# Second fetch behind the weight residues on GpSimd, down casts 2 and 3 one product group later

## Chip, cores and metric

One NeuronCore of a Trainium2 chip runs the whole program. The metric is device microseconds of one execution; lower is better.

## What is computed

Four layers act on x of 4 batches by 512 rows by 512 columns: a graph attention, a mixture of eight experts with two of them for each row, an attention on a normalized score matrix, and a feed-forward layer in which a hidden value survives only if it is among the two largest of its four. The change touches the program of the last two:

```
    def _L1_xattn_ref(p, k_v, W_k, b_k, ln_gamma, ln_beta):
...
        kv = k_v @ W_k.T + b_k
        out = jnp.einsum('bij,bjd->bid', p, kv)
        sim = jnp.einsum('bid,bjd->bij', out, kv) * scale
        mu = jnp.mean(sim, axis=-1, keepdims=True)
        var = jnp.var(sim, axis=-1, keepdims=True)
        sim = (sim - mu) * jax.lax.rsqrt(var + EPS) * ln_gamma + ln_beta
        attn = jax.nn.softmax(sim, axis=-1)
        return attn
...
        h = jax.nn.silu(jnp.einsum('bsh,hi->bsi', x, w_gate)) * jnp.einsum('bsh,hi->bsi', x, w_up)
        h_sparse = _sparsify_2to4(h)
        return jnp.einsum('bsi,ih->bsh', h_sparse, w_down)
    x = x + _L0_xattn_ref(ctx_512, _layernorm(x, axis=-1), L0_xattn_W0, ...)
    x = x + _L0_ffn_ref(_layernorm(x, axis=-1), L0_ffn_gate_w, ...)
    x = x + _L1_xattn_ref(_layernorm(x, axis=-1), ctx_512, L1_xattn_W_k, ...)
    x = x + _L1_ffn_ref(_layernorm(x, axis=-1), L1_ffn_w_gate, ...)
    return x
```

## The kernel before

All matrix products are made of three: each float32 operand is split into a rounded part ("hi", cast on ScalarE) and a residue ("lo", raw minus hi), and TensorE adds hi by lo, lo by hi and hi by hi (`product3`, lines 76 to 78).

The feed-forward layer (`ffn`) runs in 16 **units** n = 0 to 15. A unit is one batch of 512 rows by one quarter of the 2048 hidden columns. In a unit TensorE makes four **product groups** r = 0 to 3, each a gate and an up product for 128 hidden columns (24 matmuls), and then the down product of the unit before, in four row tiles (48 matmuls). Two consecutive units at a batch border use the same quarter, so there are 13 weight sets: units 4, 8 and 12 bring no new one (`starts(n)` is false for them).

A set has four gate/up pieces (512 KB each) and four down pieces (256 KB each). A piece is loaded by SyncE's queue into one of two raw slots, cast on ScalarE (`act_gate_up` line 1391, `act_down` line 1399) and its residue is made on GpSimd (`pool_gate_up` line 1403, `pool_down` line 1409). The residue frees the slot. SyncE issues in the order of its program and waits before each load for the residue two pieces back. In a unit with both kinds its order is: down 2, down 3, next set's down 0, down 1, then gate/up 2, gate/up 3, next set's gate/up 0, 1.

In unit n the down pieces of set `SPLIT[n - 1]` are prepared if unit n - 1 started it, and the gate/up pieces of the set that unit n + 1 starts. So units 1, 2, 4, 6, 8, 10, 12 and 14 prepare both, units 3, 7, 11 and 15 down alone (unit 15 its own set's down pieces too), units 5, 9 and 13 gate/up alone.

On VectorE a unit has the four hidden products (line 1449), then `keep_two` for each half of the rows: ScalarE takes magnitudes (`size`, line 2419), VectorE makes three compares (line 2510), eight tallies (2516 to 2523) and four mask multiplies (2526). Then ScalarE rounds the hidden tiles (2426) and VectorE makes their residues (2532) at the start of the next unit. `evac` (2545) adds a down tile to x.

Between these, the attention of batches 1 to 3 (and the last part of the expert layer for them) is done in halves of 256 rows, by `later`, in slots 6n to 6n + 5 of unit n, under a plan. For half h the steps fall so: in unit 2h - 1, slot 6n + 1 the first fetch of expert rows from DRAM on GpSimd (`fetch(pool, h, 0)`) and in slot 6n + 2 the first add on VectorE and the second fetch into the same buffer, which waits for that add; in unit 2h the second add and the statistics (slot 6n), GpSimd's power for 1/deviation (`pool_rstd`, line 2093), ScalarE's norm (line 2140), TensorE's transposes (line 2115) ahead of group 3, the context product behind group 3 and the similarity product between the halves of the down product; in unit 2h + 1 the score normalization, exponentials (line 2157), the probability add (line 2227), and the second norm and its transposes.

Of the kernel before, what the change touches and what calls it, by code (L numbers as in the profile page):

```python
# [30 lines left out]
Q, RQ = I // (4 * P), 4  # L31
# [2215 lines left out]
def ffn(nc, outer, dram, out):  # L2247
# [3 lines left out]
    with ExitStack() as ctx:  # L2251
# [3 lines left out]
        u, later = outer["units"], outer["later"]  # L2255
# [19 lines left out]
        def due(name, slot):  # L2275
            return plan.get((name, slot), ())

        def starts(n):
            return n < UNITS and FIRST[SPLIT[n]] == n

        with nc.Block() as block:
# [40 lines left out]
            @block.gpsimd  # L2322
            def _(pool):
                def slot_work(slot):
                    for h in due("centre", slot):
                        later.pool_rs(pool, h)
                    for h in due("add1", slot):
                        later.pool_rstd(pool, 0, h)
                    for h in due("prob", slot):
                        later.pool_rstd(pool, 1, h)  # L2330
                    for h in due("fetch0", slot):
                        later.fetch(pool, h, 0)
                    for h in due("add0", slot):
                        later.fetch(pool, h, 1)

                for r in range(2, RQ):
                    u.pool_gate_up(pool, 0, r)
                    slot_work(r - 1)
                slot_work(RQ - 1)
                for r in range(RQ):  # L2340
                    u.pool_gate_up(pool, 1, r)
                for n in range(1, UNITS):
                    down = (SPLIT[n - 1],) if starts(n - 1) else ()
                    gate = (SPLIT[n + 1],) if starts(n + 1) else ()
                    for s in down:
                        u.pool_down(pool, s, 0)
                        u.pool_down(pool, s, 1)
                    slot_work(6 * n)
                    for s in down:
                        u.pool_down(pool, s, 2)  # L2350
                        u.pool_down(pool, s, 3)
                    for s in gate:
                        u.pool_gate_up(pool, s, 0)
                    slot_work(6 * n + 1)
                    for s in gate:
                        u.pool_gate_up(pool, s, 1)
                    slot_work(6 * n + 2)
                    for s in gate:
                        u.pool_gate_up(pool, s, 2)
                    slot_work(6 * n + 3)  # L2360
                    for s in gate:
                        u.pool_gate_up(pool, s, 3)
                if starts(LAST):
                    for r in range(RQ):
                        u.pool_down(pool, SPLIT[LAST], r)
# [32 lines left out]
            def _(act):  # L2398
                def early(slot):
                    for h in due("turn0", slot):  # L2400
                        later.act_hi(act, 0, h)
                    for h in due("context", slot):
                        later.act_o_hi(act, h)
                    for h in due("turn1", slot):
                        later.act_hi(act, 1, h)
# [9 lines left out]
                def size(n, k):  # L2415
                    act.wait_ge(u.hid_made, RQ * (n + 1))
                    if 2 * n + k >= 1:
                        act.wait_ge(mag_free, 2 * n + k)
                    act.activation(mag[:, :, :], hid[:, :, HN * k:HN * k + HN], ACT.Abs).then_inc(mag_ready, 1)  # L2419
# [20 lines left out]
                for n in range(1, UNITS):  # L2440
                    down = (SPLIT[n - 1],) if starts(n - 1) else ()
                    gate = (SPLIT[n + 1],) if starts(n + 1) else ()
                    for r in range(RQ):
                        early(6 * n + r)
                        u.act_silu(act, n, r, sg)
                        if r == 0:
                            round_hid(n - 1)
                        for s in gate:
                            if r >= 1:
                                u.act_gate_up(act, s, r - 1)  # L2450
                        for s in down:
                            if r < 2:
                                u.act_down(act, s, 2 * r)
                                u.act_down(act, s, 2 * r + 1)
                        if n == LAST and starts(n) and r >= 1:
                            u.act_down(act, SPLIT[n], r - 1)
                        late(6 * n + r)
                    early(6 * n + 4)
                    if n == LAST and starts(n):
                        u.act_down(act, SPLIT[n], RQ - 1)  # L2460
                    size(n, 0)
                    for s in gate:
                        u.act_gate_up(act, s, RQ - 1)
                    size(n, 1)
                    early(6 * n + 5)
                for k in range(2):
                    half = slice(HN * k, HN * k + HN)
# [237 lines left out]
```

## Time and profile before

| | |
|---|---|
| median of 3 runs | 1108.22 us (1106.13 to 1113.89) |
| profiled execution | 1109.6 us |
| its span | 1107.9 us |
| TensorE matmul busy | 973.3 us, 88% |
| VectorE busy | 707.0 us, 64% |
| ScalarE busy | 445.8 us, 40% |
| GpSimd busy | 387.1 us, 35% |

Times in the trace are microseconds from the span's start. The feed-forward units run from about 509 us to the end. A row of a timeline names the engine, the line of the kernel, the operation, the tiles written and read, and in brackets how long the engine stood idle before it and who ended that. PE is TensorE, DVE VectorE, ACT ScalarE, POOL GpSimd, SPq SyncE's DMA queue.

### The profile page before, as it was taken

How to read it: one execution, taken by the hardware profiler on the slowest of the kernel's cores; microseconds unless marked ns; L12 is line 12 of the kernel's file. 1: busy time of each engine (PE TensorE's matmuls, PEld its weight loads, DVE VectorE, ACT ScalarE, POOL GpSimd, SP SyncE). 2: the span in 40 equal slices, each digit the busy share in tenths (PEclk: the TensorE clock that was granted, in tenths of full speed). 3: DMA queues.
4: the chain of work that ended last, by engine and by line, in shares of the span. 5: the costliest groups of instructions: out<-in, count | busy, mean ns of one | idle time of the engine just before them, and what ended most of it. 6: DMA issues, size and time to landing. Idle time of an engine off the chain costs nothing.

```text
span 1107.9 us, 15674 instructions
## 1 busy us (share of the span) xinstructions
PE 973.3 (88%) x4615; PEld 806.6 (73%) x4616; DVE 707.0 (64%) x1436; ACT 445.8 (40%) x753; POOL 387.1 (35%) x368
## 2 busy tenths in 40 slices
PE   4996539999999996428698999998999989999997
PEld 3883339999999994216586888877888868888885
DVE  7986734422435223592678796995978959855566
ACT  4875234332434322223344345433443443433431
POOL 0465023341232302232463335244442553143530
PEclk8998759999999997558798999999999999999999
DMA  8267044452444313301341223233212421033211
GB/s 328 66 145 210 38 158 153 165 175 76 147 166 137 95 57 105 114 1 57 98 131 58 85 68 102 70 100 109 77 47 68 153 86 66 13 102 114 76 53 43
DMA packets 46237, 113.85 MB, mean 103 GB/s; under 512 B 7137, under 2 KB 7265, under 8 KB 45025
## 3 DMA queue, kind: packets, MB, share of 16 engines
q1 hardware_dynamic: 37600, 90.03, 24.4%
q0 software_dynamic: 8576, 23.08, 8.0%
q8 instruction: 30, 0.49, 0.2%
q14 instruction: 31, 0.25, 0.1%
HBM read 90.28 MB, written 22.81 MB: 102 GB/s over the span
## 4 chain that ended last, share of the span: by engine, by line
PE 34%; DVE 13%; ACT 2%; POOL 2%; issue 1%; DMA 1%; ACTq 0%; DVEq 0%
PE ps L76 11%; PE ps L78 11%; PE ps L77 11%; DVE raw L2510 3%; DVE f_hid L2526 2%; DVE kv_c_lo L2532 1%; DVE l_stats L2178 1%; DVE x L2168 1%; POOL f_w_lo L1409 1%; DVE x L2227 1%; DVE x L2545 1%; PE ps L2115 1%; DMA raw<-in_ffn_dn 1%; POOL f_w_lo L1403 1%; POOL l_rstd L2093 1%
## 5 line engine op out<-in xcount | busy, mean ns | idle before, releaser
L76 PE MATMUL ps<-f_x_lo,f_w_hi 128*128 128x512 f32 x512 | 207.1, 405 | 10.2 <-DVE f_hid L1449 4.7
L77 PE MATMUL ps<-f_x_hi,f_w_lo 128*128 128x512 f32 x512 | 204.9, 400 | 0.0
L78 PE MATMUL ps<-f_x_hi,f_w_hi 128*128 128x512 f32 x512 | 204.5, 399 | 0.0
L1403 POOL TENSOR_TENSOR f_w_lo<-raw,f_w_hi 128x1024 fp32r<-128x1024 f32 x52 | 124.9, 2413 | 68.5 <-ACT f_w_hi L1391 68.3
L1409 POOL TENSOR_TENSOR f_w_lo<-raw,f_w_hi 128x512 fp32r<-128x512 f32 x52 | 76.9, 1494 | 190.8 <-ACT f_w_hi L1399 190.8
L76 PEld LDWEIGHTS ps<-f_x_lo,f_w_hi 128*128 128x128 f32 x512 | 98.9, 193 | 34.9 <-issue 6.6
L78 PEld LDWEIGHTS ps<-f_x_hi,f_w_hi 128*128 128x128 f32 x512 | 98.7, 193 | 22.9
L77 PEld LDWEIGHTS ps<-f_x_hi,f_w_lo 128*128 128x128 f32 x512 | 99.1, 194 | 22.1
L1449 DVE TENSOR_TENSOR f_hid<-moe_rows,ps 128x512 f32<-128x512 f32 x64 | 43.8, 685 | 110.9 <-PE ps L78 67.3
L76 PE MATMUL ps<-gu_w_lo,m_xT_hi 128*128 (+1 forms) x312 | 106.2, 340 | 4.6 <-DVE m_xT_lo L1690 4.3
L76 PE MATMUL ps<-f_w_lo,kv_c_hi 128*128 128x512 f32 x256 | 101.5, 397 | 2.9 <-DVE x L2545 2.3
L77 PE MATMUL ps<-gu_w_hi,m_xT_lo 128*128 (+1 forms) x312 | 101.8, 326 | 0.0
L78 PE MATMUL ps<-gu_w_hi,m_xT_hi 128*128 (+1 forms) x312 | 101.8, 326 | 0.0
L78 PE MATMUL ps<-f_w_hi,kv_c_hi 128*128 128x512 f32 x256 | 101.0, 395 | 0.0
L77 PE MATMUL ps<-f_w_hi,kv_c_lo 128*128 128x512 f32 x256 | 100.4, 392 | 0.0
L1700 DVE TENSOR_TENSOR m_hT_lo<-ps,m_hT_hi 128x384 fp32r<-128x384 f32 x39 | 21.7, 557 | 114.4 <-ACT m_hT_hi L1641 114.4
L1443 ACT ACTIVATE moe_rows<-ps 128x512 f32<-128x512 f32 x64 | 38.2, 597 | 131.2 <-PE ps L78 131.0
L2510 DVE TENSOR_TENSOR raw<-kv_c_raw 128x768 bf16<-128x768 f32 (+2 forms) x96 | 85.3, 942 | 5.7 <-ACT kv_c_raw L2419 5.7
L76 PEld LDWEIGHTS ps<-gu_w_lo,m_xT_hi 128*128 128x128 f32 x312 | 59.5, 191 | 11.3 <-issue 5.6
L2545 DVE TENSOR_TENSOR x<-ps,x 128x512 f32<-128x512 f32 x64 | 42.4, 684 | 34.2 <-PE ps L78 34.2
L1391 ACT CAST f_w_hi<-raw 128x1024 fp32r<-128x1024 f32 x52 | 54.1, 1040 | 21.3 <-DMA raw<-in_ffn_gu 21.3
L1554 POOL TENSOR_TENSOR dn_w_lo<-raw,dn_w_hi 128x1536 f32 (+1 forms) x7 | 24.5, 3507 | 103.0 <-DVE dn_w_hi L1714 103.0
(352 smaller groups left out, 2012.6 us busy)
## 6 DMA issues: line engine op xcount, KB each, us to landing
raw<-in_ffn_gu SPq DMA_DIRECT2D x52, 512.0 KB, 3.5
raw<-in_ffn_dn SPq DMA_DIRECT2D x52, 256.0 KB, 2.6
raw<-in_moe_gu SPq DMA_DIRECT2D x32, 352.0 KB, 4.3
y_scratch<-m_y SPq DMA_DIRECT2D x39, 256.0 KB, 2.3
raw<-in_moe_dn SPq DMA_DIRECT2D x24, 256.0 KB, 4.3
x<-in_x SPq DMA_DIRECT2D x4, 1024.0 KB, 11.7
gat_rows<-g_ybuf SPq DMA_DIRECT2D x16, 256.0 KB, 3.4
xn_scratch<-g_xn SPq DMA_DIRECT2D x16, 256.0 KB, 3.9
```

What stands on the lines that cost most here:

```text
L76: eng.matmul(out, lhs_hi, rhs_lo, start=start, stop=False)
L77: eng.matmul(out, lhs_lo, rhs_hi, start=False, stop=False)
L78: return eng.matmul(out, lhs_hi, rhs_hi, start=False, stop=stop)
L1391: act.copy(self.w_hi[r][:, 0:2, :], self.raw_gu[:, r % self.SLOTS, :, :]).then_inc(self.gate_up_hi, 1)
L1403: pool.tensor_tensor(self.w_lo[r][:, 0:2, :], self.raw_gu[:, r % self.SLOTS, :, :], self.w_hi[r][:, 0:2, :].bitcast(F32), ALU.subtract).th ...
L1409: pool.tensor_tensor(self.w_lo[r][:, k, :], self.raw_dn[:, r % self.SLOTS, :], self.w_hi[r][:, k, :].bitcast(F32), ALU.subtract).then_inc( ...
L1443: act.activation(sg[:, k % 2, :], self.gate_bank(n, r), ACT.Silu).then_inc(self.silu, 1)
L1449: dve.tensor_tensor(out, sg[:, k % 2, :], self.up_bank(n, r), ALU.mult).then_inc(self.hid_made, 1)
L1554: pool.tensor_tensor(rt["dn_w_lo"][:, at], rt["raw_dn"], rt["dn_w_hi"][:, at].bitcast(F32), ALU.subtract).then_inc(dn_lo, 1)
L2510: ins = dve.tensor_tensor(beats[:, at:at + w, :], mag[:, i, :].unsqueeze(1).broadcast_to([P, w, HN]), mag[:, j0:j1, :], ALU.is_ge)
L2526: ins = dve.scalar_tensor_tensor(out=hid[:, r, half], in0=tally[:, r, :], scalar=bound, in1=hid[:, r, half], op0=op, op1=ALU.mult)
L2545: dve.tensor_tensor(X[:, t, :], u.acc(n, i), X[:, t, :], ALU.add).then_inc(u.acc_free, 1)
```

## The change

GpSimd: down residues 2 and 3 of a unit go from ahead of gate/up residue 0 to behind gate/up residue 1, and the second fetch goes from slot 6n + 2 to the unit's end, behind gate/up residue 3. ScalarE: the casts of down 2 and 3 go from group 1 to group 2; in unit 15 its own down pieces are cast in pairs, 0 and 1 at group 3, 2 and 3 behind both `size` steps. SyncE, TensorE and VectorE keep their programs.

```diff
@@ pool, slot_work
                     for h in due("fetch0", slot):
                         later.fetch(pool, h, 0)
+
+                def fetch_second(slot):
                     for h in due("add0", slot):
                         later.fetch(pool, h, 1)
@@ pool, unit loop
                         u.pool_down(pool, s, 0)
                         u.pool_down(pool, s, 1)
                     slot_work(6 * n)
-                    for s in down:
-                        u.pool_down(pool, s, 2)
-                        u.pool_down(pool, s, 3)
                     for s in gate:
                         u.pool_gate_up(pool, s, 0)
                     slot_work(6 * n + 1)
                     for s in gate:
                         u.pool_gate_up(pool, s, 1)
+                    for s in down:
+                        u.pool_down(pool, s, 2)
+                        u.pool_down(pool, s, 3)
                     slot_work(6 * n + 2)
                     for s in gate:
                         u.pool_gate_up(pool, s, 2)
                     slot_work(6 * n + 3)
                     for s in gate:
                         u.pool_gate_up(pool, s, 3)
+                    fetch_second(6 * n + 2)
@@ act, unit loop
                         for s in down:
-                            if r < 2:
-                                u.act_down(act, s, 2 * r)
-                                u.act_down(act, s, 2 * r + 1)
-                        if n == LAST and starts(n) and r >= 1:
-                            u.act_down(act, SPLIT[n], r - 1)
+                            if r in (0, 2):
+                                u.act_down(act, s, r)
+                                u.act_down(act, s, r + 1)
+                        if n == LAST and starts(n) and r == RQ - 1:
+                            u.act_down(act, SPLIT[n], 0)
+                            u.act_down(act, SPLIT[n], 1)
                         late(6 * n + r)
                     early(6 * n + 4)
-                    if n == LAST and starts(n):
-                        u.act_down(act, SPLIT[n], RQ - 1)
                     size(n, 0)
                     for s in gate:
                         u.act_gate_up(act, s, RQ - 1)
                     size(n, 1)
+                    if n == LAST and starts(n):
+                        u.act_down(act, SPLIT[n], 2)
+                        u.act_down(act, SPLIT[n], 3)
                     early(6 * n + 5)
```

GpSimd's row in units 5 and 6 before. `128x1024` is a gate/up residue, `128x512` a down residue, the DMA rows are the fetches, the first `l_rstd` row is unit 5's power, the second one R(6)'s.

```order
L2101 TENSOR_TENSOR l_rs<-l_sve,minus_half 128x1 x2
L1403 TENSOR_TENSOR f_w_lo<-raw,f_w_hi 128x1024
L2086 DMA moe_rows<-y_scratch,slot 128x512 x2
L1403 TENSOR_TENSOR f_w_lo<-raw,f_w_hi 128x1024
L2093 TENSOR_TENSOR l_rstd<-l_var_eps,minus_half 128x2
L2095 TENSOR_TENSOR l_nmean<-l_nmean,l_rstd 128x2
L2086 DMA moe_rows<-y_scratch,slot 128x512 x2
L1403 TENSOR_TENSOR f_w_lo<-raw,f_w_hi 128x1024 x2
L1409 TENSOR_TENSOR f_w_lo<-raw,f_w_hi 128x512 x2
L2093 TENSOR_TENSOR l_rstd<-l_var_eps,minus_half 128x2
L2095 TENSOR_TENSOR l_nmean<-l_nmean,l_rstd 128x2
L1409 TENSOR_TENSOR f_w_lo<-raw,f_w_hi 128x512 x2
```

The same engine and place after, from unit 5's gate/up residue 1 on:

```order
L1403 TENSOR_TENSOR f_w_lo<-raw,f_w_hi 128x1024
L2093 TENSOR_TENSOR l_rstd<-l_var_eps,minus_half 128x2
L2095 TENSOR_TENSOR l_nmean<-l_nmean,l_rstd 128x2
L1403 TENSOR_TENSOR f_w_lo<-raw,f_w_hi 128x1024 x2
L2086 DMA moe_rows<-y_scratch,slot 128x512 x2
L1409 TENSOR_TENSOR f_w_lo<-raw,f_w_hi 128x512 x2
L2093 TENSOR_TENSOR l_rstd<-l_var_eps,minus_half 128x2
L2095 TENSOR_TENSOR l_nmean<-l_nmean,l_rstd 128x2
L1403 TENSOR_TENSOR f_w_lo<-raw,f_w_hi 128x1024 x2
L1409 TENSOR_TENSOR f_w_lo<-raw,f_w_hi 128x512 x2
L1403 TENSOR_TENSOR f_w_lo<-raw,f_w_hi 128x1024 x2
```

The fetch pair has moved behind the two gate/up residues of unit 5, and in unit 6 the second down pair has moved between gate/up residues 1 and 2.

ScalarE in unit 4 (an even unit with both kinds of piece) before: `L1391` is a gate/up cast, `L1399` a down cast, `L1443` the silu of a group, `L2140` the norm, `L2147` the cast of the transposed rows, `L2151` that of the context product.

```order
L1443 ACTIVATE moe_rows<-ps 128x512
L1391 CAST f_w_hi<-raw 128x1024
L1399 CAST f_w_hi<-raw 128x512 x2
L2140 ACTIVATE moe_rows<-x,l_nmean,l_rstd 128x512 x2
L1443 ACTIVATE moe_rows<-ps 128x512
L1391 CAST f_w_hi<-raw 128x1024
L2147 CAST k_hi<-ps 128x4x128 x2
```

The same place after:

```order
L1443 ACTIVATE moe_rows<-ps 128x512
L1391 CAST f_w_hi<-raw 128x1024
L2140 ACTIVATE moe_rows<-x,l_nmean,l_rstd 128x512 x2
L1443 ACTIVATE moe_rows<-ps 128x512
L1391 CAST f_w_hi<-raw 128x1024
L1399 CAST f_w_hi<-raw 128x512 x2
L2147 CAST k_hi<-ps 128x4x128 x2
```

The two down casts have moved from ahead of the norm to ahead of the transposed rows' cast.

## Rows read from the trace of the kernel before

**Rows 1.** Busy table: PE, PEld, DVE, ACT, POOL busy us (xcount), clock, DMA share.

```profile
core 0: us, PE busy (x) PEld busy (x) DVE busy (x) ACT busy (x) POOL busy (x), PEclk, DMA share, GB/s
...
640.00:680.00 40.00, 40.00 (x183) 32.62 (x182) 34.58 (x72) 20.40 (x31) 17.22 (x16) 1.00 0.21 61
```

**Rows 2.** Timeline of TensorE: the waits in units 2, 6, 10 and 15.

```profile
595.50 0.77 PE L76 MATMUL ps<-f_x_lo,f_w_hi 128*128 128x512 f32 x1 [3.07 <-DVE f_hid L1449]
...
604.48 0.66 PE L2115 MATMUL ps<-ident,moe_rows 128*128 128x128 f32 x4 [1.68 <-ACT moe_rows L2140]
...
743.90 0.47 PE L76 MATMUL ps<-f_x_lo,f_w_hi 128*128 128x512 f32 x1 [0.73 <-DVE f_hid L1449]
...
752.90 1.97 PE L2115 MATMUL ps<-ident,moe_rows 128*128 128x128 f32 x8 [3.31 <-ACT moe_rows L2140]
...
900.79 1.36 PE L2115 MATMUL ps<-ident,moe_rows 128*128 128x128 f32 x8 [3.17 <-ACT moe_rows L2140]
...
1098.73 0.47 PE L76 MATMUL ps<-f_w_lo,kv_c_hi 128*128 128x512 f32 x1 [2.35 <-DVE x L2545]
```

**Rows 3.** Timeline of TensorE: first transposes of unit 8.

```profile
825.16 1.19 PE L2115 MATMUL ps<-ident,moe_rows 128*128 128x128 f32 x8
```

**Rows 4.** Chain of waits, unit 5 (start us, us, what).

```profile
724.36 6.45 DVE raw L2510 x3
```

**Rows 5.** Timeline of VectorE: unit 5's second compares, GpSimd idle.

```profile
736.44 1.88 DVE L2510 TENSOR_TENSOR raw<-kv_c_raw 128x768 bf16<-128x768 f32 x3
```

**Rows 6.** Timeline of GpSimd, unit 5.

```profile
721.97 1.03 POOL L2086 DMA_INDIRECT moe_rows<-y_scratch,slot  x1 [0.16 <-issue]
...
724.28 4.76 POOL L1403 TENSOR_TENSOR f_w_lo<-raw,f_w_hi 128x1024 fp32r<-128x1024 f32 x2
```

**Rows 7.** Timeline of GpSimd: the power steps, units 2, 4, 6, 8.

```profile
602.56 0.74 POOL L2093 TENSOR_TENSOR l_rstd<-l_var_eps,minus_half 128x2 f32<-128x2 f32 x1 [3.17 <-DVE l_var_eps L2184]
...
675.05 0.73 POOL L2093 TENSOR_TENSOR l_rstd<-l_var_eps,minus_half 128x2 f32<-128x2 f32 x1 [3.16 <-DVE l_var_eps L2184]
...
750.98 0.74 POOL L2093 TENSOR_TENSOR l_rstd<-l_var_eps,minus_half 128x2 f32<-128x2 f32 x1 [3.17 <-DVE l_var_eps L2184]
...
823.07 0.73 POOL L2093 TENSOR_TENSOR l_rstd<-l_var_eps,minus_half 128x2 f32<-128x2 f32 x1 [3.17 <-DVE l_var_eps L2184]
```

**Rows 8.** Timeline of ScalarE: the first norm, unit 6.

```profile
752.03 1.52 ACT L2140 ACTIVATE moe_rows<-x,l_nmean,l_rstd 128x512 f32<-128x512 f32 x2 [1.07 <-POOL l_nmean L2095]
```

**Rows 9.** Timelines of GpSimd, ScalarE and SyncE's queue, unit 4.

```profile
676.01 2.53 POOL L1409 TENSOR_TENSOR f_w_lo<-raw,f_w_hi 128x512 fp32r<-128x512 f32 x2
678.51 4.75 POOL L1403 TENSOR_TENSOR f_w_lo<-raw,f_w_hi 128x1024 fp32r<-128x1024 f32 x2
...
678.00 1.04 ACT L1391 CAST f_w_hi<-raw 128x1024 fp32r<-128x1024 f32 x1
...
684.40 1.05 ACT L1391 CAST f_w_hi<-raw 128x1024 fp32r<-128x1024 f32 x1 [2.51 <-DMA raw<-in_ffn_gu]
...
680.94 0.33 SPq L1376 DMA_DIRECT2D raw<-in_ffn_gu  x1
```

**Rows 10.** Page, DMA issues: KB each, median us from issue to landing.

```profile
raw<-in_ffn_gu SPq DMA_DIRECT2D x52, 512.0 KB, 3.5
raw<-in_ffn_dn SPq DMA_DIRECT2D x52, 256.0 KB, 2.6
```

**Rows 11.** Timeline of VectorE: first compares of units 2, 4, 6, 8.

```profile
618.14 2.79 DVE L2510 TENSOR_TENSOR raw<-kv_c_raw 128x768 bf16<-128x768 f32 x3
...
689.17 2.88 DVE L2510 TENSOR_TENSOR raw<-kv_c_raw 128x768 bf16<-128x768 f32 x3
...
766.00 2.79 DVE L2510 TENSOR_TENSOR raw<-kv_c_raw 128x768 bf16<-128x768 f32 x3
...
837.12 3.31 DVE L2510 TENSOR_TENSOR raw<-kv_c_raw 128x768 bf16<-128x768 f32 x3
```

**Rows 12.** Timeline of VectorE: first hidden tile of unit 7.

```profile
780.49 0.69 DVE L1449 TENSOR_TENSOR f_hid<-moe_rows,ps 128x512 f32<-128x512 f32 x1 [0.66 <-PE ps L78]
```

**Rows 13.** Timeline of VectorE: first compares of unit 15.

```profile
1082.70 2.13 DVE L2510 TENSOR_TENSOR raw<-kv_c_raw 128x768 bf16<-128x768 f32 x3 [0.27 <-ACT kv_c_raw L2419]
```

## The prediction

> **What bounds the kernel now.** I read the busy table by stretches first, then TensorE's waits, then the chain that ended last, then the queues around each wait. The change touches only the feed-forward units (from 509 us on). There TensorE is nearly full: one stretch of 40 us without a hole is [rows 1]. One can gain or lose only where TensorE waits. Its waits are few: 3.07 and 1.68 us in unit 2, 0.73 and 3.31 in unit 6, a pair like it in unit 10 with 3.17 as the longer, and 2.35 at the end [rows 2]. Units 4 and 8 have none: their first transpose follows a matmul with no idle time [rows 3].
>
> Units 6 and 10 wait for the second norm chain: rows added on VectorE, statistics, GpSimd's power, ScalarE's norm, the transposes. Followed back, that chain is VectorE's, and its largest piece is the compares of keep_two in unit 5: 6.45 us [rows 4]. The same three compares take 1.88 us when GpSimd is idle [rows 5]. In the 6.45 GpSimd runs two gate/up residues, 4.76 us together [rows 6], and VectorE is held for as long. So a GpSimd residue that falls on VectorE's SBUF work costs the chain its own length. This decides the sum: the change moves residues.
>
> I call R(n) the start of GpSimd's power in even unit n: 602.56, 675.05, 750.98, 823.07 for units 2, 4, 6, 8 [rows 7]; R(10) lies a step of the same length on. All of the middle is one VectorE chain from R to R. Up to R(10) each microsecond on it counts where TensorE has no slack left; behind unit 10 no later work hangs on it but the tail.
>
> **The change, part by part.**
>
> 1. *Fetch behind residues (units 1, 5, 9).* Before, two indirect fetches of some 1 us each stood between the power and gate/up residues 2 and 3, so both fell on the compares [rows 6]. Now residue 2 starts where the first fetch starts today, at 721.97 [rows 6], and is through at 724.4, just as the compares begin at 724.36 [rows 4]. Residue 3 still waits for its cast, which follows the first size step, and costs its 2.4 us. The compares take 1.9 + 2.4 = 4.3 instead of 6.45: gain 2.15 us each in units 5 and 9, 4.3 in all. The fetches then leave at about 728; VectorE adds their rows ahead of the statistics that lead to R(6) = 750.98 [rows 7], so the rest of unit 5's masking hides them, well over 10 us. If that cover went, they would cost about their landing, 2 to 3 us.
>
> 2. *Casts of down 2 and 3 one group later on ScalarE.* Before, ScalarE waits for their loads ahead of the first norm. This hid nothing: in unit 6 the norm still waited 1.07 us for GpSimd behind them [rows 8]. Gain 0. In units 3, 7 and 11 they now stand ahead of the exponentials; the table load moves by 1.1 us, of which 0.5 us and more was a wait for VectorE. Their residues leave two score steps (about 0.9 us too long today) and fall on the two probability additions instead. I take +0.25 us each in units 3 and 7.
>
> 3. *Down residues 2 and 3 behind gate/up 0 and 1 on GpSimd (units with both: 1, 2, 4, 6, 8, 10, 12, 14).* Here is the cost. SyncE's queue is in order: down 2, down 3, next down 0, next down 1, then gate/up 2. The next down loads wait for residues 2 and 3 of down, so gate/up load 2, which before waited only for gate/up residue 0, now waits for four instructions more. Unit 4: power done at 676.0, gate/up residue 0 to 678.5; cast 1 runs at 678.00 to 679.04 as before, its residue to 681.5; the two down residues, 2.53 us, to 684.0; issue at 684.3 instead of 680.94; landing 3.5 us later [rows 9, 10] at 687.8. ScalarE takes cast 2 at 687.8 instead of 684.40, and behind it stand the context cast and the first size step, 1.4 us: compares start at 690.2 instead of 689.17. GpSimd runs residues 2 and 3 from 688.9 to 693.7, and both now lie on the compares, which before met 1.0 us of them. They end at about 695.5 = R + 20.4. Before, they end at R + 18.4, 17.0, 17.8, 17.4 in units 2, 4, 6, 8 [rows 7, 11]. So the chain grows by 2.0 + 3.4 + 2.6 + 3.0 = 11.0 us. The load is now queued behind two down loads of 256 KB just issued; the trace never shows four loads at once. Bounds a unit: 0 (its fixed part runs beside theirs) and 1.8 us (512 KB land 0.9 us later than 256 KB [rows 10], so 0.9 for each of the two ahead). I take 0.4, near the lower end, since the first of them leaves 1.3 us earlier, a down residue's length: +1.6 for four units.
>
> 4. *Slack that takes some of it.* VectorE waits for TensorE 0.66 us in unit 7 [rows 12]. I read the like in units 3, 5 and 9 and take 2.1 us off for all four. The first norm of units 4 and 8 has at most 0.5 us before TensorE waits for it. Behind unit 10 no power step for units beyond hangs on the chain, and I take its delay as absorbed.
>
> 5. *Unit 1.* There is a gain of 2.15 us as in part 1, but the late gate/up load 2 also holds ScalarE's cast ahead of the norm: 1.3 to 2.6 us later. I take 0, bounds -0.4 and +1.0.
>
> 6. *Units 12 to 15.* TensorE has work throughout; the first hidden tiles of units 13 and 15 come some 3 us later and by my times still about 1 us before their banks are needed. In unit 15 ScalarE no longer waits for four down loads in a row, but the size step gains only the 0.27 us that VectorE waits for it [rows 13]; VectorE is held by TensorE's output before that. Against it, the last two down residues, 2.6 us, used to run beside the first compares and now fall on the mask multiplies. Bounds -0.3 and +2.1; I take +1.3.
>
> **Sum.** 11.0 + 1.6 - 2.1 - 4.3 + 0.5 + 0 + 1.3 = +8.0 us. The profiled execution took 1109.6 us (span 1107.9), so it would take 1117.6; against the median of 1108.22 that is 1116.2, 0.7% slower.
>
> One place where row and rule part. The trace shows VectorE held through two residues back to back [rows 4, 6], and the sum of +8.0 goes by that. The Trainium skill, page "SBUF — State Buffer", section "Who interferes with whom", says that the engine which issues first holds the shared port for one instruction and the other blocks. Read strictly, VectorE would take its turn between the two residues, and by that the sum would be near zero (rival A).
>
> **Rivals.**
>
> *A. The turns alternate, and gate/up residue 3 costs VectorE nothing where it queues (0.14).* Each residue 3 would then be paid by GpSimd, which has time. Parts 3 and 1 lose 2.4 us a unit in units 2, 4, 6, 8: 8.0 - 9.6 = -1.6, or 1107. Against it: VectorE's stretch of SBUF work after the compares is longer than the residue can wait, and the 4.76 us for two residues shows GpSimd losing nothing. The rule named above would give this.
>
> *B. The gain stands and the loads come in time (0.08).* If gate/up load 2 lands before ScalarE asks (the cast at 684.40 waited 2.51 us for it even now [rows 9]), part 3 is zero: -4.3 in units 5 and 9, -2.15 in unit 1, and up to 2 us of slower matmuls behind each of the three long waits, since after 3.31 us of idle the eight transposes took 1.97 us against 1.19 [rows 2, 3]. That gives 1096 to 1102. It needs SyncE not to be in order, against [rows 9].
>
> *C. The late load reaches TensorE (0.20).* Behind the cast on ScalarE stands also the context cast, on which the similarity matmuls between the two halves of the down products depend. They come 5.6 us after the context, and o_lo is ready about 1.4 us before them in my times. If the load lands more than 1.4 us later than I take, TensorE stops and its clock drops, in units 4 and 8, and each later load counts fully on the chain in four units: 8.0 + 4 x 1.2 = +13, or 1121.
>
> *D. Nothing to be seen (0.13).* VectorE's slack between R and R is larger than I read, and gain and loss cancel: 1108, give or take 3.
>
> **How the numbers follow.** The forecast, +4 to +12, has 0.45. No change and a difference of 1% (11 us) can just be told apart by a measurement of this kernel. Faster by more than that needs the far end of B: 0.05. Slower by more needs C or the upper end of the forecast: 0.22. The rest, 0.73, lies within 1%. The range 1104 to 1122 leaves out most of B and the far end of C.
>
> **What the profile will show.** Right: compares of 4.2 to 4.4 us in units 5 and 9; in units 4 and 8 ScalarE's gate/up cast 2 some 3.5 us later after a wait for a DMA, compares above 4.5 us, and a new TensorE wait of 1 to 2 us before the transposes; waits in 6 and 10 as long as before or a little longer. Wrong: cast 2 of the even units where it was, or compares there still near 3 us. The forecast also fails if a power step is held on GpSimd by a residue queued ahead of it.

## The result, and the profile after

The changed kernel takes 1122.2 us (median of 6 runs, 1120.0 to 1124.4) against 1107.9 of the kernel before beside it (6 runs): a ratio of 1.0126, 95% interval 1.0097 to 1.0155, so 11 to 17 us slower. The profiled execution took 1122.3 us, its span is 1120.6 (before 1107.9). The ratios in this document leave out two slow executions, one of the kernel before (1277.5 us) and one of e10 (1576.8 us).

The page's busy line and its chain, of the kernel after:

```profile
PE 975.1 (87%) x4615; PEld 803.9 (72%) x4616; DVE 720.1 (64%) x1436; ACT 442.3 (39%) x753; POOL 392.4 (35%) x368
DVE 26%; PE 15%; POOL 4%; ACT 3%; DMA 3%; issue 3%; SPq 0%; ACTq 0%; DVEq 0%
```

VectorE is busy 13 us longer than before with the same 1436 instructions, and its share of the chain is 26%, where it was 13%. Some of its instructions are held while they run, and the rows below show by what.

The power steps R(2) to R(10) on GpSimd, in the timeline of after (those of before are in [rows 7]):

```profile
600.55 0.74 POOL L2093 TENSOR_TENSOR l_rstd<-l_var_eps,minus_half 128x2 f32<-128x2 f32 x1 [3.17 <-DVE l_var_eps L2184]
676.07 0.74 POOL L2093 TENSOR_TENSOR l_rstd<-l_var_eps,minus_half 128x2 f32<-128x2 f32 x1 [3.17 <-DVE l_var_eps L2184]
754.62 0.73 POOL L2093 TENSOR_TENSOR l_rstd<-l_var_eps,minus_half 128x2 f32<-128x2 f32 x1 [3.16 <-DVE l_var_eps L2184]
829.90 0.73 POOL L2093 TENSOR_TENSOR l_rstd<-l_var_eps,minus_half 128x2 f32<-128x2 f32 x1 [3.17 <-DVE l_var_eps L2184]
907.89 0.73 POOL L2093 TENSOR_TENSOR l_rstd<-l_var_eps,minus_half 128x2 f32<-128x2 f32 x1 [3.17 <-DVE l_var_eps L2184]
```

R(2) comes 2.0 us earlier than in [rows 7], R(10) 9.0 us later (before at 898.87), the end 12.7 us later. So unit 1 gains 2, units 2 to 9 lose 11.0, the tail loses 3.7.

**Where part 1 gained.** Unit 5, against [rows 4] and [rows 6]:

```profile
730.33 4.11 DVE L2515 TENSOR_TENSOR raw<-kv_c_raw 128x768 bf16<-128x768 f32 x3 [1.53 <-ACT kv_c_raw L2422]
...
727.75 2.38 POOL L1403 TENSOR_TENSOR f_w_lo<-raw,f_w_hi 128x1024 fp32r<-128x1024 f32 x1
731.31 2.85 POOL L1403 TENSOR_TENSOR f_w_lo<-raw,f_w_hi 128x1024 fp32r<-128x1024 f32 x1 [1.19 <-ACT f_w_hi L1391]
```

Residue 2 is over when the compares begin (730.13 and 730.33); residue 3 alone falls on them, and 6.45 us became 4.11.

**Where part 3 lost.** Unit 4, against [rows 9], [rows 11] and [rows 3]: SyncE's issues, ScalarE's cast 2, GpSimd, the compares, and a TensorE wait.

```profile
683.82 1.58 SPq L1382 DMA_DIRECT2D raw<-in_ffn_dn  x2
685.44 0.91 SPq L1376 DMA_DIRECT2D raw<-in_ffn_gu  x2
...
691.06 1.05 ACT L1391 CAST f_w_hi<-raw 128x1024 fp32r<-128x1024 f32 x1 [8.32 <-DMA raw<-in_ffn_gu]
...
692.19 5.46 POOL L1403 TENSOR_TENSOR f_w_lo<-raw,f_w_hi 128x1024 fp32r<-128x1024 f32 x2 [7.15 <-ACT f_w_hi L1391]
...
693.37 5.16 DVE L2515 TENSOR_TENSOR raw<-kv_c_raw 128x768 bf16<-128x768 f32 x3 [0.53 <-ACT kv_c_raw L2422]
...
692.89 0.50 PE L76 MATMUL ps<-k_lo,l_o_hi 128*128 128x512 f32 x1 [1.06 <-DVE l_o_lo L2196]
```

Gate/up load 2 leaves at R + 9.4, the cast starts at R + 15.0 after 8.3 us of waiting for it, and both residues lie on the compares. TensorE stops 1.06 us for o_lo, the residue of the context product. In units 2, 4, 6 and 8 the second compares start 2.5, 5.4, 2.8 and 4.6 us later against R than before, 15.3 us together.

How the two residues hold the compares is seen when each instruction stands by itself. Unit 4 after (the first two compares, the second residue):

```profile
693.37 2.02 DVE L2515 TENSOR_TENSOR raw<-kv_c_raw 128x768 bf16<-128x768 f32 x1 [0.53 <-ACT kv_c_raw L2422]
695.32 2.88 DVE L2515 TENSOR_TENSOR raw<-kv_c_raw 128x512 bf16<-128x512 f32 x1
...
694.54 3.11 POOL L1403 TENSOR_TENSOR f_w_lo<-raw,f_w_hi 128x1024 fp32r<-128x1024 f32 x1
```

The first residue ends at 694.58. The first compare ends 0.81 us later, while the second residue waits (3.11 us in place of 2.41). So VectorE has one turn between the two residues. The second compare is then held until the second residue is done at 697.65: 2.88 us in place of 0.68. Unit 5 of the kernel before is the other case:

```profile
724.36 5.50 DVE L2510 TENSOR_TENSOR raw<-kv_c_raw 128x768 bf16<-128x768 f32 x1 [0.86 <-ACT kv_c_raw L2419]
...
726.63 2.41 POOL L1403 TENSOR_TENSOR f_w_lo<-raw,f_w_hi 128x1024 fp32r<-128x1024 f32 x1
```

Here the first compare has no turn: the second residue follows the first at its usual 2.41 us, and the compare ends 0.82 us behind both.

**Part 2, the surprise.** Unit 3: one score step on VectorE, the two down residues on GpSimd, the exponential that waits for it.

```profile
641.34 3.68 DVE L2218 SCALAR_TENSOR_TENSOR kv_c_raw<-kv_c_raw,l_rs,k_beta 128x512 f32<-128x512 f32 x1
...
641.92 2.54 POOL L1409 TENSOR_TENSOR f_w_lo<-raw,f_w_hi 128x512 fp32r<-128x512 f32 x2
...
645.78 0.72 ACT L2157 ACTIVATE kv_c_raw<-kv_c_raw,l_nmax 128x512 f32<-128x512 f32 x1 [3.33 <-DVE l_nmax L2220]
```

The two score steps of this unit take 0.74 and 3.68 us; before they took 1.28 and 1.06. It is the residues that hold the second one and not the fetches ahead of them: the first score step, at 639.97, ran beside a fetch (639.61 to 640.64) and took its usual 0.74.

**The tail.** Unit 15's mask multiplies beside the last two down residues, and TensorE's last two waits, against [rows 13] and the last row of [rows 2]:

```profile
1095.79 3.53 DVE L2531 SCALAR_TENSOR_TENSOR f_hid<-raw,f_hid 128x256 f32<-128x256 bf16 x4
...
1101.71 0.50 PE L76 MATMUL ps<-f_w_lo,kv_c_hi 128*128 128x512 f32 x1 [2.01 <-DVE kv_c_lo L2543]
1109.88 0.47 PE L76 MATMUL ps<-f_w_lo,kv_c_hi 128*128 128x512 f32 x1 [2.32 <-DVE x L2550]
```

The mask multiplies took 1.44 us before, and the first of these waits was 0.52. A table by stretches of the end (busy us of TensorE, its loads, VectorE, ScalarE, GpSimd, then the granted clock):

```profile
1106.00:1110.00 4.00, 1.68 (x8) 1.09 (x7) 2.89 (x6) 1.05 (x1) 0.00 (x0) 1.00 0.00 0
1111.30:1114.60 3.30, 3.30 (x9) 2.52 (x9) 0.34 (x1) 0.00 (x0) 0.00 (x0) 0.50 0.40 147
1115.00:1119.00 4.00, 2.24 (x10) 1.49 (x8) 0.69 (x1) 0.00 (x0) 0.00 (x0) 1.00 0.22 82
```

Behind waits of 2.01 and 2.32 us TensorE's granted clock is 0.50 (1.2 GHz) for some 3.5 us: its matmuls start 0.43 us apart, not 0.23. Before, the two waits were 0.52 and 2.35 us and the matmuls behind them kept 0.23.

### The profile page after: what moved, and what is told of

It is laid out like the page before. It is cut to its first block, busy times and chain, and to the rows that moved or that the text cites. A ratio compares the mean times of both kernels' runs of the same rounds, so it can differ in the third digit from the quotient of the medians.

```text
span 1120.6 us, 15674 instructions
## 1 busy us (share of the span) xinstructions
PE 975.1 (87%) x4615; PEld 803.9 (72%) x4616; DVE 720.1 (64%) x1436; ACT 442.3 (39%) x753; POOL 392.4 (35%) x368
## 4 chain that ended last, share of the span: by engine, by line
DVE 26%; PE 15%; POOL 4%; ACT 3%; DMA 3%; issue 3%; SPq 0%; ACTq 0%; DVEq 0%
DVE raw L2515 6%; PE ps L76 5%; PE ps L78 5%; PE ps L77 5%; DVE f_hid L2531 3%; DMA raw<-in_ffn_gu 3%; DVE kv_c_lo L2537 3%; POOL f_w_lo L1403 2%; DVE x L2550 1%; POOL f_w_lo L1409 1%; DVE kv_c_raw L2218 1%; DVE f_hid L1449 1%; DVE x L2168 1%; DVE l_stats L2178 1%; ACT kv_c_raw L2422 1%
## 5 line engine op out<-in xcount | busy, mean ns | idle before, releaser
L1403 POOL TENSOR_TENSOR f_w_lo<-raw,f_w_hi 128x1024 fp32r<-128x1024 f32 x52 | 130.7, 2521 | 97.3 <-ACT f_w_hi L1391 97.1
L77 PEld LDWEIGHTS ps<-f_x_hi,f_w_lo 128*128 128x128 f32 x512 | 97.9, 191 | 21.5
L2515 DVE TENSOR_TENSOR raw<-kv_c_raw 128x768 bf16<-128x768 f32 (+2 forms) x96 | 94.6, 1038 | 15.8 <-ACT kv_c_raw L2422 15.8
L1443 ACT ACTIVATE moe_rows<-ps 128x512 f32<-128x512 f32 x64 | 38.0, 594 | 102.1 <-PE ps L78 101.9
L1391 ACT CAST f_w_hi<-raw 128x1024 fp32r<-128x1024 f32 x52 | 54.1, 1040 | 56.5 <-DMA raw<-in_ffn_gu 56.5
L76 PEld LDWEIGHTS ps<-f_w_lo,kv_c_hi 128*128 128x128 f32 x256 | 48.4, 189 | 17.0 <-DVE kv_c_lo L2543 5.2
```

What stands on the lines that cost most here:

```text
L76: eng.matmul(out, lhs_hi, rhs_lo, start=start, stop=False)
L77: eng.matmul(out, lhs_lo, rhs_hi, start=False, stop=False)
L1391: act.copy(self.w_hi[r][:, 0:2, :], self.raw_gu[:, r % self.SLOTS, :, :]).then_inc(self.gate_up_hi, 1)
L1403: pool.tensor_tensor(self.w_lo[r][:, 0:2, :], self.raw_gu[:, r % self.SLOTS, :, :], self.w_hi[r][:, 0:2, :].bitcast(F32), ALU.subtract).th ...
L1443: act.activation(sg[:, k % 2, :], self.gate_bank(n, r), ACT.Silu).then_inc(self.silu, 1)
L2515: ins = dve.tensor_tensor(beats[:, at:at + w, :], mag[:, i, :].unsqueeze(1).broadcast_to([P, w, HN]), mag[:, j0:j1, :], ALU.is_ge)
```

## The experiments

Each ratio is to the kernel before, run beside it on the same chip. "Us to before" is the ratio less 1, times 1108; times given as "measured" are medians. The last two columns come from the profiled run: us from R(2) to R(10), and from R(10) to the end of the span.

| kernel | ratio (95%) | us to before | R(2) to R(10) | tail |
|---|---|---|---|---|
| before | | | 296.3 | 209.0 |
| after | 1.0126 (1.0097 to 1.0155) | +14.0 | 307.3 | 212.7 |
| e1 fetch alone | 0.9946 (0.9933 to 0.9959) | -6.0 | 292.2 | 210.3 |
| e2 down edits alone | 1.0175 (1.0161 to 1.0189) | +19.4 | 310.8 | 212.8 |
| e3 gate/up loads first | 0.9971 (0.9958 to 0.9984) | -3.2 | 296.0 | 209.0 |
| e4 units 3, 7, 11 old, 15 in part | 1.0080 (1.0065 to 1.0095) | +8.9 | 302.7 | 212.0 |
| e12 their casts old | 1.0125 (1.0107 to 1.0143) | +13.9 | 307.6 | 214.0 |
| e13 their residues old | 1.0095 (1.0076 to 1.0115) | +10.5 | 301.5 | 213.9 |
| e9 late, not queued | 1.0057 (1.0038 to 1.0077) | +6.3 | 303.3 | 211.2 |
| e5b unit 15 old | 1.0134 (1.0110 to 1.0158) | +14.8 | 307.6 | 215.7 |
| e11 loads first from 10 | 1.0094 (1.0072 to 1.0117) | +10.4 | 307.7 | 210.0 |
| e8 e3 + old places | 0.9935 (0.9916 to 0.9954) | -7.2 | 290.5 | 208.6 |
| e7 e1 + loads first | 0.9944 (0.9923 to 0.9965) | -6.2 | 291.2 | 210.7 |
| e10 e8 + cast 3 later | 0.9970 (0.9957 to 0.9983) | -3.3 | 293.4 | 210.7 |

### The two halves of the change apart: e1, e2

e1 is the kernel before with `fetch_second(6 * n + 2)` behind gate/up residue 3. e2 is the changed kernel with the fetch back in its slot.

> The kernel before with one edit of the change alone: the second fetch behind gate/up residue 3 on GpSimd. Theory (a residue that falls on the compares costs the chain its length, and the fetches had put two on them): compares of units 1, 5 and 9 shrink by one residue, 2.15 us each, so about 6 us less than before, 1102 us (1100 to 1104), and the even units keep their compares of 2.8 to 3.3 us. Rival (the chain has slack, or the later rows cost as much): 1108, within 1.5 us. Second rival (the time lost in the changed kernel comes from the fetch itself, which leaves too late): slower than before, 1110 or more.

> The changed kernel with the second fetch back in its old slot, so only the edits of the down residues and casts. Theory: these carry the whole loss and the fetch's gain is missing, so about 6 us above the changed kernel: 1128 us (1125 to 1131). Rival (the two parts meet in the same place, the residues wait anyway): 1122, as the changed kernel. Rival (the fetch is at fault): below 1119.

Measured: 1103.3 us and 1129.5 us (before beside them 1109.6). The fetch is worth -6.0 us put on the kernel before and -5.4 (1.0126 less 1.0175) put on the other half: the parts add, within the intervals. In e1 the compares are 4.10 us in units 1, 5 and 9, as expected; of the even units' only two are within the expected 2.8 to 3.3 (2.79 and 3.08 in units 2 and 6), units 4 and 8 have 3.44 and 4.05. R(2) to R(10) is 4.1 us shorter. The whole loss is in the down edits.

### Is it the late load? e3, e9

```diff
 # SyncE, unit loop, on the changed kernel (e3; e9 has the two lines marked + + more)
 down(s, 2); down(s, 3)
-down(s + 1, 0); down(s + 1, 1)
+ + if both kinds in this unit:
+ +     sp.wait_ge(u.down_lo, RQ * SPLIT[n - 1] + 4)
 gate_up(s', 2); gate_up(s', 3)
+down(s + 1, 0); down(s + 1, 1)
 gate_up(s' + 1, 0); gate_up(s' + 1, 1)
```

> The changed kernel with one edit on SyncE: gate/up loads 2 and 3 are issued ahead of the next set's down 0 and 1. Theory (in units 2, 4, 6 and 8 the loss is the late gate/up load 2, which waits behind loads that wait for down residues 2 and 3): cast 2 of the even units comes back to some R + 8 to 9, the compares start at R + 14 again and take under 4.5 us, landing about 3.5 us; units 2, 4, 6, 8 give back 2.5 to 3.3 us each: 1110 us (1107 to 1113). Rival (it is the order of the residues on GpSimd, two more of them ahead of gate/up residue 2, that counts): within 2 us of the changed kernel, 1120 to 1124.

> The changed kernel with gate/up loads 2 and 3 ahead of the next set's down loads, but made to wait for down residue 3 of the unit, so that they leave as late as in the changed kernel and with no down load just ahead of them. Theory (two costs: the late issue, and 1.1 to 2.5 us of landing behind two down loads): landing 3.5 us in units 2, 4, 6, 8 and 1.1 to 2.5 us back in each, 1116.5 us (1115 to 1118.5). Rival (it is the two gate/up loads issued half a microsecond apart that share the engines, the downs count little): landing stays at 4.6 us or more, 1121 to 1123.

Measured: 1106.7 and 1116.0 us. e3 in unit 4, where R is at 674.66 (SyncE, cast 2, GpSimd's down residues 2 and 3 and gate/up residue 2, the compares):

```profile
678.02 3.48 SPq L1376 DMA_DIRECT2D raw<-in_ffn_gu  x2
...
681.71 1.05 ACT L1391 CAST f_w_hi<-raw 128x1024 fp32r<-128x1024 f32 x1 [0.37 <-DMA raw<-in_ffn_gu]
...
681.10 2.56 POOL L1409 TENSOR_TENSOR f_w_lo<-raw,f_w_hi 128x512 fp32r<-128x512 f32 x2
683.62 2.41 POOL L1403 TENSOR_TENSOR f_w_lo<-raw,f_w_hi 128x1024 fp32r<-128x1024 f32 x1
...
688.62 2.79 DVE L2516 TENSOR_TENSOR raw<-kv_c_raw 128x768 bf16<-128x768 f32 x3
```

GpSimd has the same order as in the changed kernel, but the load leaves at R + 3.4, its cast is at R + 7.1, and the compares are 2.79 us again. That alone is worth 17.2 us by the ratios (1.0126 less 0.9971; 15.6 by the two profiled spans), more than the whole loss and a little more than its expectation allowed; the rival that blamed the residues' order is out. The load leaves even sooner than in the kernel before (R + 5.9), but the second compares of units 2, 4, 6 and 8 start within 0.5 us of where they did: 22.8, 21.2, 22.6 and 21.3 us behind R, before 22.8, 21.5, 22.3 and 21.8.

e9 in unit 4, R at 675.27:

```profile
684.29 0.80 SPq L1376 DMA_DIRECT2D raw<-in_ffn_gu  x2
...
687.77 1.05 ACT L1391 CAST f_w_hi<-raw 128x1024 fp32r<-128x1024 f32 x1 [5.81 <-DMA raw<-in_ffn_gu]
```

Here the loads leave at R + 9.0, late as in the changed kernel, and the cast follows 3.5 us behind the issue instead of 5.6. In units 2, 4, 6, 8 cast 2 comes 0.8, 2.5, 0.6 and 0.2 us sooner than after (R + 12.6, 12.5, 12.6, 14.2 against 13.4, 15.0, 13.2, 14.4), of which 0.36 each is that the load no longer waits for the issue of the second down load. From R(2) to R(10) that gives 4.0 us; the rest of the late load, from e9 to e3, is 7.4. Landing did not return to 3.5 us everywhere (5.2 in unit 8), so the expectation's span of 1.1 to 2.5 us a unit was too much. The rival (the two gate/up loads share the engines, 1121 us or more) is out by the 1116.0.

### Which edit lengthens the score step? e4, e12, e13

All on the changed kernel. In units 3, 7 and 11, e4 sets both back, e12 ScalarE's casts of down 2 and 3 (group 1), e13 GpSimd's residues (ahead of the first fetch). e4's edit reaches unit 15 too, which its expectation doesn't say: there down 2 and 3 of the set that unit 14 starts are cast one group earlier. So e4 is read from R(2) to R(10).

> The changed kernel, but in the units that prepare down pieces alone (3, 7, 11) casts and residues of down 2 and 3 as before. Theory (the residues fall back to back on one score step of VectorE, 3.68 us in place of 0.74, which the next wait of ScalarE shows): about 2 us back in each of units 3 and 7, 1118 us (1116.5 to 1119.5). Rival (0.25 us a unit, as the prediction had it): 1121.7, not to be told from the changed kernel.

> The changed kernel, but in units 3, 7 and 11 ScalarE casts down 2 and 3 one group earlier, as before; GpSimd's order stays changed (fetches ahead of the two residues). Theory (it is the place behind the two fetches that puts both residues on one score step): the score step stays at 3.7 us, 1122 us (1120.5 to 1123.5). Rival (it is the late casts): the step falls to about 1.3 us and 1.5 to 2 us come back in each of units 3 and 7, 1118.5 us.

> The changed kernel, but in units 3, 7 and 11 GpSimd makes down residues 2 and 3 ahead of the first fetch, as before; ScalarE's casts stay late. Theory (the place behind the two fetches is at fault): the residues start one by one behind their casts, the first under the hidden product and the reduction, the two score steps take 2.4 to 3 us together in place of 4.4, and 1.5 to 2 us come back in each of units 3 and 7: 1118.5 us (1117 to 1120). Rival (the late casts): 1122.

Measured: 1117.8, 1123.1 and 1119.5 us. Unit 3 of e12, then of e13:

```profile
641.72 3.67 DVE L2218 SCALAR_TENSOR_TENSOR kv_c_raw<-kv_c_raw,l_rs,k_beta 128x512 f32<-128x512 f32 x1
...
641.31 0.96 POOL L2086 DMA_INDIRECT moe_rows<-y_scratch,slot  x1 [0.30 <-issue]
642.30 2.53 POOL L1409 TENSOR_TENSOR f_w_lo<-raw,f_w_hi 128x512 fp32r<-128x512 f32 x2
```

```profile
639.51 0.75 DVE L2218 SCALAR_TENSOR_TENSOR kv_c_raw<-kv_c_raw,l_rs,k_beta 128x512 f32<-128x512 f32 x1
640.89 1.12 DVE L2218 SCALAR_TENSOR_TENSOR kv_c_raw<-kv_c_raw,l_rs,k_beta 128x512 f32<-128x512 f32 x1
...
640.18 3.00 POOL L1409 TENSOR_TENSOR f_w_lo<-raw,f_w_hi 128x512 fp32r<-128x512 f32 x2 [1.20 <-ACT f_w_hi L1399]
```

The casts' place does nothing (13.9 against 14.0). The residues' place does: behind the two fetches (1.0 us each) they begin inside the second score step and hold it to their end, 3.67 us; ahead of the fetches they begin 0.7 us before the step, under the reduction of the row's maximum, and the two steps take 1.87 together. From R(2) to R(10) e4 gives back 4.6 us and e13 5.8. By the ratios e4 is worth 5.1 us and e13 3.4, and e13's is not clear of noise against the changed kernel; that e13 differs from e12, which ran beside it, is. The tails of e12 and e13 are 1.3 and 1.2 us longer: TensorE waits for a hidden tile 1.48 us in unit 13 of e12, 0.64 and 0.66 in units 13 and 15 of e13, and 0.45 in the changed kernel. Why these waits differ is open.

### The tail: e5b, e11

e5b is the changed kernel with unit 15 as before. e11 has the load order of e3 from unit 10 on.

> The changed kernel with unit 15 entirely as before: the casts and residues of its down pieces 2 and 3 and of its own set's four. Theory 1 (the tail's loss sits in unit 15's mask multiplies, which two residues lengthen from 1.4 to 3.5 us): 2.1 to 3.7 us less than the changed kernel, 1119.5 us. Theory 2 (in the run with the loads first the stretch from unit 10's power step to the end came back to 209.0 us although unit 15 was the changed one, so the loss sits in units 10, 12 and 14): 0.4 us less or nothing, 1122 (1120.8 to 1123).

> The changed kernel with gate/up loads 2 and 3 first on SyncE from unit 10 on alone. Theory 2 (the tail lost its time to the late loads of units 10, 12 and 14, whose compares take 5.2 to 5.5 us): about 3.7 us less than the changed kernel, 1118.5 us (1117.5 to 1120), and power step of unit 10 to the end back at 209 us. Theory 1 (unit 15): 1122.

Measured: 1124.8 us (before beside it 1110.5) and 1120.6. Setting unit 15 back gains nothing that the intervals show (1.0134 against 1.0126). Its mask multiplies are back to 1.43 us, but ScalarE again casts one down piece a group and waits for each load, and its gate activations now hold TensorE:

```profile
1090.95 0.50 PE L76 MATMUL ps<-f_x_lo,f_w_hi 128*128 128x512 f32 x1 [2.23 <-ACT moe_rows L1443]
```

That is a wait inside unit 15's groups that neither kernel has. ScalarE waits for these loads as long as in the kernel before (at most 3.36 and 3.30 us); why that reaches TensorE only here isn't shown. e11 gives 3.5 us by the ratios, which is within their intervals, and 2.7 in its profile. Its mask multiplies still take 3.52 us and TensorE still waits 2.00 us behind them. It saves 1.2 us ahead of that wait, which its edit can claim, and 1.5 us behind it, where the stretch at the lower clock is missing. That stretch can't be put down to the edit: of the profiled runs with waits of 2.0 and 2.3 us there, those of e2, e12 and e13 have it too, and that of e4 doesn't. So neither theory was whole. The tail's 3.7 us are, row by row, 1.5 of longer wait behind the mask multiplies, 0.45 of a new wait in unit 13, 1.5 of matmuls at the lower clock in that execution, and 0.2 of small change; the first is unit 15's edit, and by e5b undoing it there costs as much at the casts.

### Together: e8, e7, e10

e8 is e3 with units 3, 7, 11 and 15 as before. e7 is e1 with the load order of e3. e10 is e8 with `act_gate_up(act, s, RQ - 1)` behind `size(n, 1)`.

> Three edits together: gate/up loads 2 and 3 first on SyncE, units 3, 7 and 11 as before, unit 15 as before; left of the change are the second fetch and the order of the residues in the units that prepare both kinds. Theory (the parts add up): 1106.7 with the loads first, less 4.4 for units 3 and 7, less 2 for the tail: 1100 us (1099 to 1102), ahead of the fetch edit alone at 1103.3 since the even units' compares are 2.8 us in all of them. Rival (VectorE's chain is no longer the bound there, so the gains overlap): 1103 to 1105.

> The kernel before with the second fetch moved and gate/up loads 2 and 3 first on SyncE, nothing else. With the residues in the old order gate/up load 2 still leaves only behind gate/up residue 0, which follows down residues 2 and 3, so its issue stays and only the down loads ahead of it go. Theory: landing stays near 3.5 us, 1103 us (1101.5 to 1104.5), as the fetch edit alone. Rival (less queueing shows there too): 1101 or less.

> The combination of the run with old places and loads first, and gate/up cast 3 behind the second size step instead of ahead of it. Theory (a residue costs VectorE its length only on work between two SBUF tiles, and little under work that reads PSUM): residue 3 leaves the compares (2.8 becomes 1.9 us, 4.1 becomes 1.9) and falls partly on the last mask multiplies and partly on the residues of the transposes and the adds of down tiles, which read PSUM; 0.5 to 1.5 us a unit, 1097 us (1094 to 1100). Rival (the mask multiplies grow by all that the compares lose): 1100, as without it. Rival (the later cast frees its slot later and the next set's loads come late): 1103 or more.

Measured: 1102.1, 1101.9 and 1106.3 us. e8, e7 and e1 beat the kernel before by 0.54 to 0.65% and can't be told apart. In e8 TensorE waits for 1.95 and 1.96 us in units 6 and 10 and nowhere else between 610 and 1090 us: VectorE's chain has little left to give. That this is why e8 took 1102 us and not 1100 is my reading, not tested. In unit 4 of e8 (first fence) and e10 (second) one sees what is held and what is not:

```profile
688.26 0.69 DVE L2555 TENSOR_TENSOR x<-ps,x 128x512 f32<-128x512 f32 x1 [3.42 <-PE ps L78]
688.87 0.41 DVE L2196 TENSOR_TENSOR l_o_lo<-ps,l_o_hi 128x256 fp32r<-128x256 f32 x1
689.20 2.79 DVE L2520 TENSOR_TENSOR raw<-kv_c_raw 128x768 bf16<-128x768 f32 x3
...
687.84 2.40 POOL L1403 TENSOR_TENSOR f_w_lo<-raw,f_w_hi 128x1024 fp32r<-128x1024 f32 x1 [1.41 <-ACT f_w_hi L1391]
```

```profile
688.45 1.89 DVE L2520 TENSOR_TENSOR raw<-kv_c_raw 128x768 bf16<-128x768 f32 x3
...
692.23 3.62 DVE L2536 SCALAR_TENSOR_TENSOR f_hid<-raw,f_hid 128x256 f32<-128x256 bf16 x4
...
692.50 2.41 POOL L1403 TENSOR_TENSOR f_w_lo<-raw,f_w_hi 128x1024 fp32r<-128x1024 f32 x1 [7.12 <-ACT f_w_hi L1391]
```

In e8 residue 3 has run for 1.36 us when the compares begin: 0.42 while VectorE is idle, the rest beside two instructions that read PSUM and take their usual time. It reaches 1.04 us into the compares and costs them 0.90. In e10 it misses that cover and falls whole on the mask multiplies, which take 3.62 in place of 1.43. My theory that it would end under the adds behind them was wrong: it starts 0.27 us after the mask multiplies do and holds them until it is done. So unit 4 loses 2.19 us there and gains 0.90. The rival of late loads has no part between 600 and 890 us: there no gate/up cast of e10 waits for its load. The Trainium skill, page "SBUF — State Buffer", section "Who interferes with whom", says that a VectorE instruction with at most one SBUF input, outside the modes that use both ports, does not contend with GpSimd, and that one with two contends with a GpSimd instruction that reads SBUF. The trace agrees, with these rows (0.69 and 0.41 us against 2.79 and 3.62).

## Why the prediction was right in kind and short in size

It said slower, by 8 us; it was 12.7 in the profiled executions and 14.0 by the ratio. 1122.2 us lies at the upper end of the range, 1122, and outside the forecast's own +4 to +12, which had 0.45. The direction was no luck. That the total stayed near the range owes something to luck: unit 1 gained 2.0 us, for which the prediction had 0.

| step of the prediction | forecast | measured, from |
|---|---|---|
| part 3, late load and both residues, less the slack of part 4 | +11.0 - 2.1 = +8.9 | +7.4 (e9 to e3, R(2) to R(10)) |
| part 3, load queued behind two down loads | +1.6 | +4.0 (after to e9) |
| part 1, fetch, units 5 and 9 | -4.3 | -4.1 (before to e1) |
| part 2, score steps in units 3 and 7 | +0.5 | +4.6 (after to e4) |
| part 5, unit 1 | 0 | -2.0 (R(2), before to after) |
| part 6, tail | +1.3 | +3.7 (after R(10)) |
| sum | +8.0 | +13.6, where the spans differ by 12.7 |

- **Right.** The chain from R to R sets the time, and a microsecond on it counts. SyncE's order carries two down residues into gate/up load 2: forecast to leave at R + 9.3 in unit 4, it left at R + 9.4. Both residues land on the compares, 5.16 us in place of 2.88. Units 5 and 9 gained what was forecast. The shape of the waits was right: 4.11 us of compares, cast 2 of unit 4 at 691.06 after a wait for a DMA, 5.6 us later against R than in [rows 9] (forecast 3.5), TensorE waits of 0.60 and 0.74 us before the transposes of units 4 and 8 (forecast 1 to 2, so shorter).
- **The step that was most off is part 2**: "I take +0.25 us each". It counted the residues' own time and had them fall on the two probability additions. It did not ask what VectorE does at the moment in which they start: behind the two fetches that is inside a score step. e13 and e12 show that this place is the cause and the casts' place is not. Measured: +4.6 us for units 3 and 7, not +0.5.
- **The queue** was put near its lower end, 0.4 us. It is 1.0 us a unit on the chain, inside the bounds of 0 and 1.8, and 0.36 of that is the issue of the second down load. The landing in unit 4 took 5.6 us, 2.1 more than 3.5 and outside the bounds.
- **A reading.** The prediction says that load 2 "now waits for four instructions more". By its own rows GpSimd made down residues 2 and 3 ahead of gate/up residue 0 before too [rows 9], so it is one residue more, gate/up 1. That takes 2.41 us, and the wait for its cast (0.74) and the issue of the second down load make it the 3.5 by which the load leaves later. The times in the prediction were right all the same.
- **The slack** of part 4 was put at 2.1 us. The second compares of units 2, 4, 6 and 8 came 15.3 us later in all, where part 3 with its queue had 12.6; late load and queue together cost 11.4 on the chain (after to e3). The difference of some 4 us was slack, by subtraction, so two errors cancelled in part.
- **Unit 1** gained 2.0 us. The late load did reach ScalarE there (cast 2 waits 6.19 us), but with no late load, in e1 and e3, R(2) comes 28.3 us after unit 1's own power step and in the changed kernel 28.8 (before 30.6): it costs 0.5 us, not 2.15. 0.2 of the 2.0 lies ahead of unit 1.
- **The tail** was forecast on VectorE alone. The mask multiplies grew by 2.1 us, of which 1.5 reached TensorE's wait, and in the profiled execution the lower clock took as much again; a clock that falls was priced in rival B and not here.
- **The rivals.** A's price is out, its mechanism is not. VectorE does get a turn between the two residues in unit 4, but the compares still pay for both, 5.16 us in place of 1.88: the residue that waited for one compare holds the next. The rule that the prediction quotes from the Trainium skill, page "SBUF — State Buffer", section "Who interferes with whom", holds for that turn. What failed is the step from it to "costs VectorE nothing where it queues" and to 1107. In unit 3, where the second residue goes ahead of a score step that already waits, the trace does not follow it. B and D are out by the result. C named the right number, 1121, and the right place: TensorE does wait for o_lo, 1.06 us in unit 4 and 0.42 in unit 8. The granted clock stayed at 1.00 in the stretches behind both waits (690 to 704 and 844 to 852 us), though, and this is not what brought the excess: the late load with all it does costs 11.4 us from R(2) to R(10), where the forecast had 10.5 and C 15.3 or more. The excess is part 2's and the tail's.

## What to carry to other kernels

When a step moves on one engine, follow each queue in program order to what it now waits for: here two GpSimd instructions moved, and the loss came from a load on SyncE that stood behind other loads that wait for them. The cheap mend was in that queue: loads that the chain needs first, prefetches behind. And for each GpSimd instruction that moves, look at which VectorE instruction it will start beside: here it was free beside one that reads PSUM (0.69 and 0.41 us, e8) or has one input (the reduction, 0.69 us in unit 3 of the kernel before, with a residue under way). Started inside one with two SBUF inputs it cost about its own length (2.19 us for 2.41 in e10), and in unit 3 the one queued behind it counted too (2.94 us for the two, which take 2.54).

## What the runs showed that I had not expected

- VectorE's score step had run 0.58 us of its usual 0.74 when the GpSimd residue began (641.34 and 641.92), and yet it ended only after both residues, at 645.02. Where a residue was under way first (e13), the step has its turn behind that one: 1.12 us for the step, and the second residue takes 1.75 in place of 1.29. The start decides, as far as all the profiled runs show. A score step or compare that starts 0.5 us or more after the first of two residues ends between them (0.55 or 0.82 us behind the first). One that starts 0.08 us after it, or 0.58 before it, ends as much behind the second. At 0.39 us both occur (unit 11 of after, unit 1 of e2). Why this is so stays open.
- A 512 KB load that lands in 3.5 us (issue to the cast that waits for it) landed in 3.9 to 5.6 us behind two 256 KB loads, and the spread from unit to unit (0.2 to 2.5 us saved by e9) has no cause that I found.
- The same two TensorE waits at the end (2.0 and 2.3 us, 8 us apart) were followed by some 3.5 us at a granted clock of 0.50 in the profiles of after, e2, e12 and e13 and by full clock in those of e4 and e11. In e3 the clock fell to 0.50 already behind the first wait (2.01 us); there the second wait was 0.79 us and the tail no longer for it (209.0). A profile's tail can thus carry 1.5 us that no edit explains, and single profiles don't tell smaller things apart there.
